# Matmuls of a cleared tile in TensorE's first two waits of a decoder layer

## The reference

```python
h  = layernorm(x)
xi = rmsnorm(h @ down_w + down_b, norm1_w)            # 128 -> 64 channels
o1 = window_attention(xi[..., :32], window=10, ...)   # shifted, 8 heads of 4
o2 = window_attention(xi[..., 32:], window=20, ...)
y  = h + concat(o1, o2) @ up_w + up_b
x  = x + y + gelu(rmsnorm(y) @ ffn_w1 + ffn_b1) @ ffn_w2 + ffn_b2
# second part: causal attention of layernorm(x) to a context with one shared matrix
q = layernorm(x) @ Wq.T;  k = v = ctx @ Wq.T
x = x + softmax(causal(q @ k.T / sqrt(128))) @ v
# third part: a mixture of 8 experts (top 2) and one shared expert
x = x + shared(layernorm(x)) + sum_e w_e * expert_e(layernorm(x))
```

## Time and profile before

| what | value |
|---|---|
| time, median of 3 runs | 193.19 us (192.81, 193.19, 193.59) |
| profiled execution, own time | 193.48 us |
| its span, first to last instruction | 191.7 us |
| instructions | 3278 |
| mean granted clock of TensorE | 0.96 |
| PE busy | 162.4 us, 85% |
| PEld busy | 130.8 us, 68% |
| DVE busy | 119.6 us, 62% |
| ACT busy | 85.4 us, 45% |
| POOL busy | 27.7 us, 14% |
| share of the chain that ended last | PE 71%, DVE 11%, ACT 6%, DMA 5% |

### The profile page before, as it was taken

One profiled execution on the slowest core, in us unless ns is written; L12 is line 12 of the kernel. 1 busy time (PEld: TensorE's weight loads), 2 busy tenths in 40 slices (PEclk: granted clock), 3 DMA queues, 4 the chain that ended last, 5 costly groups with the idle time before them and its releaser, 6 DMA issues.

```text
span 191.7 us, 3278 instructions
## 1 busy us (share of the span) xinstructions
PE 162.4 (85%) x1280; PEld 130.8 (68%) x1280; DVE 119.6 (62%) x299; ACT 85.4 (45%) x141; POOL 27.7 (14%) x37
## 2 busy tenths in 40 slices
PE   0809989999959998558877869999999999999992
PEld 0804855598848565547555648878879897979981
DVE  6184998696995989963762774655425663624423
ACT  2032261751002326007656567859690775253250
POOL 2059300007600510020132200000002000000000
PEclk9999855999997999999999999999999999999998
DMA  5999500000000000000000000000000002000001
GB/s 145 251 235 334 139 0 3 0 3 3 0 0 0 0 0 5 0 0 0 0 0 0 5 0 0 3 0 0 0 3 0 0 0 58 1 2 3 0 2 55
DMA packets 6475, 5.99 MB, mean 31 GB/s; under 512 B 1009, under 2 KB 5563, under 8 KB 6460
## 3 DMA queue, kind: packets, MB, share of 16 engines
q1 hardware_dynamic: 5260, 5.17, 10.4%
q10 hardware_dynamic: 1200, 0.62, 1.2%
HBM read 5.26 MB, written 0.52 MB: 30 GB/s over the span
## 4 chain that ended last, share of the span: by engine, by line
PE 71%; DVE 11%; ACT 6%; DMA 5%; issue 3%; SPq 2%; POOL 1%; DVEq 0%; POOLq 0%
PE ps L1081 65%; DMA wq_sb<-in_wq 5%; ACT hid L622 2%; DVE ox L847 2%; PE ps L1315 2%; DVE prod L820 2%; DVE prod L790 2%; PE ps L1107 1%; DVE prod L827 1%; DVE stat L836 1%; ACT L622 1%; ACT L609 1%; ACT L586 1%; ACT xcT L556 1%; DVE prT L915 1%
## 5 line engine op out<-in xcount | busy, mean ns | idle before, releaser
L1081 PE MATMUL ps<-moe_w_sb,hid 128*128 128x128 f32 x288 | 34.8, 276 | 0.1
L1081 PEld LDWEIGHTS ps<-moe_w_sb,hid 128*128 128x128 f32 x288 | 33.7, 192 | 1.3 <-ACT hid L622 0.5
L622 ACT ACTIVATE hid<-ps,cols_sb 128x512 f32<-128x512 f32 x36 | 24.5, 687 | 22.5 <-PE ps L1081 22.2
L990 DVE SCALAR_TENSOR_TENSOR acc<-ps,wts,acc 128x128 f32<-128x128 f32 x72 | 20.3, 344 | 20.8 <-PE ps L1081 20.6
L1081 PE MATMUL ps<-prod,half_ident 128*128 128x400 f32 x36 | 16.8, 596 | 0.8 <-ACT winT L490 0.8
L1081 PE MATMUL ps<-xf_hi,w_hi 128*128 128x512 f32 x36 | 16.2, 449 | 1.4 <-ACT hid L622 1.1
L1081 PE MATMUL ps<-prod,ident 128*128 128x200 f32 x70 | 12.7, 335 | 2.5 <-DVE prod L827 2.2
L1081 PE MATMUL ps<-xf_lo,w_hi 128*128 128x512 f32 x36 | 14.2, 395 | 0.0
L1081 PE MATMUL ps<-xf_hi,w_lo 128*128 128x512 f32 x36 | 14.1, 392 | 0.0
L1081 PEld LDWEIGHTS ps<-prod,ident 128*128 128x128 f32 x70 | 11.7, 190 | 2.9 <-DVE prod L827 2.3
L790 DVE TENSOR_TENSOR prod<-qkv 128x800 f32<-128x800 f32 (+1 forms) x16 | 13.1, 867 | 0.1
(11 more groups left out here) (140 smaller groups left out, 271.0 us busy)
## 6 DMA issues: line engine op xcount, KB each, us to landing
moe_w_sb<-in_moe_w SPq DMA_DIRECT2D x1, 1152.0 KB
xT_sb<-in_x_t SPq DMA_DIRECT2D x1, 512.0 KB, 3.9
ctxT_sb<-in_ctx_t SPq DMA_DIRECT2D x1, 512.0 KB, 7.7
out<-acc SPq DMA_DIRECT2D x8, 64.0 KB, 1.6
hid<-in_bias SPq DMA_DIRECT2D x1, 369.7 KB
x_sb<-in_x ACTq DMA_DIRECT2D x1, 320.0 KB, 7.5
ffn_w_sb<-in_ffn_w SPq DMA_DIRECT2D x2, 128.0 KB, 6.2
x_sb<-in_x ACTq DMA_DIRECT2D x1, 192.0 KB, 8.6
```

The source lines that it names most:

```text
L622: act.activation(hid[:, k % 2, c, :], ps[:, c, :], ACT.Gelu, bias=cols_sb[:, i:i + 1]).then_inc(moe_h_ready, 1)
L990: dve.scalar_tensor_tensor(acc[:, g, :], ps[:, 2 + k % 2, t * D:(t + 1) * D], wts[h][:, t, e:e + 1], acc[:, g, :], ALU.mult, ALU.add).then ...
L1081: return pe.matmul(dst, lhs, rhs, start=start, stop=stop)
```

## The change

A function `idle_columns(n)` is added to TensorE's program and called twice: with 2 ahead of the wait for down_sb, and with 4 ahead of the wait for the keys' inputs. It waits until GpSimd has cleared the first tile pu and then issues n matmuls of 128x512. Both operands are the cleared tile, and the result goes into bank 6 of PSUM, which nobody reads before the keys overwrite it. Nothing else is edited.

```diff
--- before.py
+++ after.py
@@ -1081,6 +1081,14 @@
                 return pe.matmul(dst, lhs, rhs, start=start, stop=stop)
 
 
+            def idle_columns(n):
+
+                pe.wait_ge(cleared, 1)
+                zeros = pu[0][:].rearrange("p i d -> p (i d)")
+                for _ in range(n):
+                    mm(ps[:, 6, :], zeros[:, 0:P], zeros)
+
+            idle_columns(2)
             pe.wait_ge(ld_down, 16)
             mm(ps[:, 7, 0:DI], down_sb[:, DI:DI + P], down_sb[:, 0:DI]).then_inc(setup_ps, 1)
 
@@ -1092,6 +1100,7 @@
                     last = mm(ps[:, 1 - n, at:at + DI], xT_sb[:, t * P:(t + 1) * P], downc[:])
                 last.then_inc(xi_ps, 1)
 
+            idle_columns(4)
             pe.wait_ge(ld_ctx, 48)
             for a in range(2):
                 last = mm(ps[:, 6 + a, :], wqT_sb[:], ctxT_sb[:, a * 512:(a + 1) * 512])
```

## The result

| | before | changed |
|---|---|---|
| time, median (range), us | 193.0 (192.78 to 193.59, 4 runs) | 195.3 (193.86 to 195.75, 4 runs) |
| profiled execution, own time, us | 193.48 | 193.86 |
| its span, us | 191.7 | 192.0 |
| mean granted clock, profiled | 0.960 | 0.938 |
| instructions | 3278 | 3302 |

The ratio is 1.0119, with a 95% interval of 1.0075 to 1.0163: the change makes the kernel about 1.2% slower. A second measurement, on another chip, gave 1.0196 (1.0144 to 1.0248). The forecast was 192.2 us, a gain. The profiled execution is the fastest of the four; the others had a mean clock of 0.929 or 0.930.

What follows compares the result with a forecast made beforehand. The early chain was bound by a load until 14.07 us, then TensorE's keys and transposes at low clock. First piece 0, second minus 0.97, the rest 0: 192.51 from 193.48, or 192.2 against the median; range 191.0 to 193.9.

Steps and rivals of the forecast that it cites:

- the clock's low stretch: TensorE at half clock from 22.81 to 33.05 us; claimed to keep its length and be carried along, price 0.
- The two matmuls ahead of the first load, price 0: Start of TensorE's program: they run 1.34 to 4.91 us, covered by the wait for down_sb, cost 0.
- an end of the range: Early case: the clock rises before 9.41 us, keys start when their data lands, gain 1.6 us at most.
- The four matmuls in front of the keys: TensorE from 9.41 us: eight passes raise the clock, end at 15.5, and the copy to winT starts at 18.1.
- T = (W + 19.65) / 2: Time the keys end and the transposes start, given the clock's rise; forecast 17.2 us instead of 17.68.
- W: Time at which TensorE's clock rises during the four added matmuls; 14.5 to 15.1 us, taken as 14.8.
- The lag: Stretch of TensorE busy without a hole before the clock rises: 5.3, 5.7 and 5.1 us in the trace.
- the 17.4 that I gave as the earliest: Earliest start of the copy to winT, since VectorE finishes the second xi product only at 17.44 us.
- The gain of 0.97: Copy to winT on VectorE at 18.1 us instead of 19.07, carried through to the end of the kernel.
- Behind the copy VectorE has work without a gap: From the copy to 33.08 us VectorE is busy, so the copy's gain carries on; what lies behind adds 0.
- That a cleared tile does not raise the clock: Slower rival: four matmuls stay at low clock, keys 2.1 us late, copy at 21.04, 195.2 us; chance 0.14.
- The rival in which the gain is given back to the clock: No-difference rival: later clock rises stay put, or the first comes at 16; 192.7 to 193.3 us, chance 0.24.

Runs made afterwards that it cites:

- again: The changed kernel unaltered, measured once more on another chip against the kernel before: ratio 1.0196, median 195.93 us.
- second_only: The changed kernel with only the four wide matmuls in front of the keys: ratio 1.0142 to the kernel before, median 195.56 us.
- second_pad144: Only the four wide matmuls, plus 36 tiny ones (144 instructions) ahead of the first load: ratio 0.9965 to the kernel before, median 192.10 us.
- first_only: The changed kernel with only the two wide matmuls ahead of the first load: ratio 1.0112 to the kernel before, median 196.33 us.
- change_pad232: The changed kernel plus 58 tiny matmuls (232 instructions) behind the four wide ones: ratio 0.9998 to the kernel before, median 193.43 us.
- change_pad136: The changed kernel plus 34 tiny matmuls (136 instructions) behind the four wide ones: ratio 1.0015 to the kernel before, median 193.84 us.
- gap_first: Kernel before plus 40 tiny matmuls, with a hand-made wait for GpSimd in the first qkv group: ratio 0.9974 to the kernel before, 192.85 us.
- second_pad144_b: second_pad144 measured once more on another chip: ratio 0.9982 to the kernel before, median 192.87 us.

## Why the prediction was wrong

**The step that failed** is in the change part by part: the added matmuls were priced by the time that they hold TensorE, and all behind the copy was put at nothing, the clock's low stretch at "price 0". What they add besides is 24 instructions ahead of everything else. They move the place at which TensorE runs out of code from behind the second group of qkv rows into it, where 0.7 to 1.3 us of stall is open in five profiles of five, in place of 0.34 or none. A stall of 0.73 us made by hand there costs 1.3%, as much as the change lost at first (1.2%) and less than at the second measurement (2.0%); with the position put back, the change is at 0.9998 and 1.0015. In the profiles most of that cost is not the stall itself but a low stretch of the clock at 78 to 92 us, 3.8 us when it comes in full, and it came more often with a stall; what links the two stays open. The trace had the sign of the gap: one idle time put down to "issue" at 44.83, between 160 small passes and the value sum. I read the groups' durations and not that gap.

**The two matmuls ahead of the first load, price 0**: right, TensorE was free at 4.91, as worked out. That they could raise the clock I had allowed for as an end of the range; they did in the first profile, and not in the second, where the x product took its 3.65 us again.

**The four matmuls in front of the keys**: the formula T = (W + 19.65) / 2 held. With the first piece without effect (again) the clock rose at 13.80, for which it gives 16.7, and the transposes began at 16.78; in second_only it rose at 12.21, which gives 15.9, and they began at 15.91. The lag was mis-sized: W was forecast at 14.8 and measured at 13.80 (again), 12.21 (second_only), 13.38 and 13.64 (second_pad144 and its repeat). The copy came at 17.84 and 17.60, against 18.1 forecast, and at 16.73 in second_only, ahead of the 17.4 that I gave as the earliest: that bound, xi on VectorE, was itself one execution's.

**The gain of 0.97** compared with one execution. Two more profiles of the kernel before have the copy at 18.03 and 17.70 with no added work. Against them the copy at 17.60 and 17.84 is between 0.4 us earlier and 0.1 later. That fits the 0.2 to 0.4% at which the second piece was measured where its instructions do no harm, in place of 0.5%.

**"Behind the copy VectorE has work without a gap"**: the copy's 1.23 us were 0.5 at the first half_ident sum. The first group of qkv rows began 1.2 us earlier (18.75 against 19.97) but ended only 0.5 earlier (24.66 against 25.18), since it holds the gap of 0.42 us; the transposes, and ScalarE's copies that the sums wait for, come behind it.

**The rivals.** That a cleared tile does not raise the clock is refuted: it rose at 5.46 us, with little else done than such matmuls. The time came out at 195.3 us where that rival said 195.2; that is luck, since the mechanism was another. The rival in which the gain is given back to the clock was nearest to the truth: low stretches do move from execution to execution, and they carry most of the loss. But it had no cause for them to become likelier. The Trainium skill ("TensorE: Matmul & The Clock Gate", Part 1) says that the time of the rise is not fixed relative to the program; the traces agree, with 16.64, 17.08 and 19.40 us for one kernel. What it says of transposes (Part 4) was not tested.

## What to carry to other kernels

Instructions put into an engine's idle time may not be free if a fast group of small ones comes later: find out where the code pieces end, look for idle time put down to "issue" inside a group that waits for nothing, and test any such insertion against fillers that restore the position. A stall is worth what it delays at its own place, so make one by hand before blaming it, and make it at a second place too. And where the clock's times are drawn anew in each execution, take three profiles of the kernel before, before a microsecond of one of them is counted as to be had.

## What the runs showed of the hardware

- TensorE's code came in transfers of 16 KB. At the gaps it went on 1.2 to 1.6 us after the transfer had ended (ten gaps in seven profiles), and the gaps stand 512 instructions apart (450 and 962), at the same count in every profile that shows them.
- The granted clock rises for matmuls of a cleared tile too: at 5.46 (after), 5.71 (first_only) and 4.98 (change_pad232), with little but two such matmuls ahead. In the profiles of again and change_pad136 the same two did not.
- A 32x1 float32 matmul, four instructions, holds TensorE for 0.11 us ahead of the first rise (40 in 4.42 us in gap_first, 36 in 3.99 in second_pad144_b), more than the 0.064 that I had reckoned.
- In one kernel's three profiles the clock first rose at 16.64, 17.08 and 19.40 us, for a time of 194.75, 191.08 and 193.48.
- The same work, from the hT product near 70 us to the first xf_hi product, took 34.8 us with no low stretch in it (7 profiles), 35.5 with 3.4 us of one (4) and 38.6 to 38.8 with 10.2 us (6).
